# Self and cross attention of a fused block as one pipeline of four phases, with weights prepared a phase ahead

## The chip, the cores and the metric

The kernel runs on one core of a Trainium2 chip. The metric is the device time of one launch in microseconds (us). A core has five engines, each with its own queue of instructions that it works through in order: TensorE (PE, its weight loads shown as PEld), VectorE (DVE), ScalarE (ACT), GpSimd (POOL) and SyncE (SP), which here only starts transfers. An engine waits at an instruction until the semaphore that it names has reached a number, and everything behind that instruction waits with it.

## The reference

The input is 2048 tokens (32 sequences of 64) of 256 numbers. Five steps follow one another, the last four of them on a layer norm of the residual:

```
x = x + wkv(layernorm(x), ctx)                       # a recurrence along time
x = x + ternary_ffn(layernorm(x))                    # hidden 704, weights rounded to -1, 0, 1
x = x + attention(layernorm(x), ctx):                # 16 query heads, 8 key/value heads, head size 128
      q  = ln(fp8(h) @ wq)    k  = ln(fp8(h) @ wk)     v  = fp8(h) @ wv        # self
      qx = ln(fp8(h) @ wqx)   kx = ln(ctx @ wkx)       vx = ctx @ wvx          # cross
      cat = [softmax(q k^T / sqrt(128)) v, softmax(qx kx^T / sqrt(128)) vx]    # 32 heads
      out = fp8(cat / smooth) @ wproj * scale
x = x + routed_ffn(layernorm(x))                     # top 2 of 8, capacity 64
```

Keys and queries are normalised head by head. The mean over a head is taken out of the weights beforehand: every head's 128 weight columns of wq, wk, wqx and wkx are multiplied by their scale and then lose their mean ("centred"). Every weight is also split into two fp32r parts, upper and lower, whose products are added, which keeps the precision.

## The kernel before, in words

The stages run one after another, each a block with a barrier at its end: wkv, ternary FFN, the LN and quantisation stage that writes the fp8 activations `xq8`, self attention, cross attention, routed FFN.

**Weights before.** All six chunks of the self weights (q in two halves, k, v, the projection in two halves; 128 x 2048 each) are prepared during the ternary stage. ACT scales each head of q and k and sums it (`self_weights_act`, L653, 48 heads). POOL centres, copies the upper part and subtracts for the lower part (`self_weights_pool`, L664; the subtraction is in `lower_part`, L642, recorded as L645). Meanwhile DVE normalises `tf_z` (L812), rounds the ternary weights (L816 to L818), takes maxima (L825) and scales `tf_z` again (L831); the first unit of the ternary FFN (L851) comes behind all of that in DVE's queue. The cross weights are loaded during self attention; ACT and POOL scale and centre one head (`cross_head_act` L706, `cross_head_pool` L715) with six of every eight units. Splitting them into upper and lower parts is the start of the cross stage (`cross_weights_act` L723, `cross_weights_dve` L730), and TensorE waits for it at L1409.

**Attention.** Each of the two stages is a software pipeline over 64 units. A unit is one tile of 128 tokens (two sequences) and two key/value groups, so four query heads; four units make a tile. Step s of every engine works on units of different age. In TensorE's queue a step is: output products of unit s-4 (L1430, from `pT` and `v`), query transposes of s-2 (L1441), projection of s-5 (L1453, from `cat`), key and value products of s (L1417; L1477 in cross), key transposes of s-2 (L1487), query products of s (L1417 again), transposes of the probabilities of s-3 (L1499), scores of s-2 (L1507). ACT's step ends with the square of the query of s (L1394), `pT` (L1397), the copy of v (L1400) and, in self, the cross head (L711 and the read of its accumulator). DVE's step begins with the sum of squares of s-1 (L1251) and ends with `tb` of s-4 (L1292). POOL's step is: `pn` of s-3 (L1214), every fourth step the conversion of the next tile (L1195), `cat` of s-4 (L1228), and last the head (L718 for the sum, L720 for the weights). The projection gathers four units in PSUM; after every fourth DVE adds the tile to the residual (L1347). Steps are written once in a hardware loop of eight units, with the first round and the tail written out.

Of the kernel before, what the change touches and what calls it, by code (L numbers as in the profile page):

```python
# [100 lines left out]
def build_program(nc, x, ctxT, params, w1T, w3T, w2T, wqT, wkT, wvT, wqxT, wkvxT, wprojT, routerT,  # L101
                  fw1T, fw2T, fb2, out):
    ctx = ExitStack()
    with ctx:
# [26 lines left out]
        with ExitStack() as held:  # L131


            work = [sb(f"w_work{i}", [P, KC * G * D], F32, held) for i in range(3)]
            tok["tw"] = ternary_weights(tok, work, held)
            stage = tok["stage_sem"] = StageSems(nc)
            wkv_stage(tok, x, ctxT, params, (w1T, w3T, w2T))
            aw = attention_weights(tok, held)
            stage = tok["stage_sem"] = stage.follow()
            ternary_ffn_stage(tok, aw, self_chunks(tok, aw, wqT, wkT, wvT, wprojT))  # L140
            xq8 = sb("xq8", [P, 4 * KC, TOK], BF16, held)
            stage = tok["stage_sem"] = stage.follow()
            ln_quant_stage(tok, xq8, work)
            stage.follow()
            cross_w = cross_chunks(tok, aw, wqxT, wkvxT, wprojT)
            attention_stage(tok, "self", xq8, aw, work, cross_w, ctxT)
            attention_stage(tok, "cross", xq8, aw, work, cross_w, ctxT)
# [419 lines left out]

def attention_weights(k, stack):


    nc, sem = k["nc"], k["sem"]

    def pair(name, shape):
        return [stack.enter_context(nc.sbuf_tensor(f"{name}{p}", shape, F32R)) for p in range(2)]

    return dict(
        q=pair("wq", [P, KC, NH * D]), k=pair("wk", [P, KC, G * D]), v=pair("wv", [P, KC, G * D]),
        p=pair("wp", [P, NH, C]),
        sums=stack.enter_context(nc.sbuf_tensor("w_sums", [P, 3, NH], F32)),
        scales=stack.enter_context(nc.sbuf_tensor("w_scales", [P, 4 * KC], F32)),  # L580
        arrived=[sem(f"w_arrived{i}") for i in range(6)], scales_ready=sem("w_scales_ready"),
        sums_ready=sem("w_sums_ready"), scaled=sem("w_scaled"), centred=sem("w_centred"), upper=sem("w_upper"),
        lower_pool=sem("w_lower_pool"), lower_dve=sem("w_lower_dve"))


class Chunk:

    def __init__(self, pair, pick, src, centred=False, scales=()):  # L590
        self.src, self.centred, self.scales = src, centred, scales
        self.upper, self.lower = (pick(t) if len(pick(t).shape) == 2 else pick(t).rearrange("p a n -> p (a n)")
                                  for t in pair)

    def scale_of(self, head):
        return self.scales[head * len(self.scales) // NH]


def heads_of(w):
    return w.rearrange("p (h d) -> p h d", d=D)  # L600


def proj_chunks(aw, wprojT, row0):
    half = NH // 2
    return [Chunk(aw["p"], lambda t, a=a: t[:, a * half:(a + 1) * half, :],
                  wprojT[row0 + a * half * D:row0 + (a + 1) * half * D, :].rearrange("(c p) n -> p c n", p=P))
            for a in range(2)]


def self_chunks(k, aw, wqT, wkT, wvT, wprojT):  # L610
    def scale(kind, h):
        return aw["scales"][:, kind * KC + h:kind * KC + h + 1]

    def halves(w):
        return w.rearrange("(h p) n -> p h n", p=P)

    q = [Chunk(aw["q"], lambda t, h=h: t[:, h, :], wqT[h * P:(h + 1) * P, :], True, [scale(0, h)])
         for h in range(KC)]
    return q + [Chunk(aw["k"], lambda t: t[:], halves(wkT), True, [scale(1, h) for h in range(KC)]),
                Chunk(aw["v"], lambda t: t[:], halves(wvT), False, [scale(2, h) for h in range(KC)])  # L620
                ] + proj_chunks(aw, wprojT, 0)


def cross_chunks(k, aw, wqxT, wkvxT, wprojT):
    kv = wkvxT.rearrange("(h p) n -> p h n", p=P)
    q = [Chunk(aw["q"], lambda t, h=h: t[:, h, :], wqxT[h * P:(h + 1) * P, :], True,
               [aw["scales"][:, 3 * KC + h:3 * KC + h + 1]]) for h in range(KC)]
    return q + [Chunk(aw["k"], lambda t: t[:], kv[:, :, 0:G * D], True),
                Chunk(aw["v"], lambda t: t[:], kv[:, :, G * D:2 * G * D])] + proj_chunks(aw, wprojT, NH * D)


def load_weights(sp, aw, work, chunks, wait_free, first=0, last=6):
    for i in range(first, last):
        c = chunks[i]
        if i >= len(work):
            wait_free(i - len(work))
        w = work[i % len(work)][:]
        dst = w if len(c.src.shape) == 2 else w.rearrange("p (a n) -> p a n", a=c.src.shape[1])
        sp.dma_start(dst, c.src).then_inc(aw["arrived"][i], 16)


def lower_part(eng, aw, work, chunks, i, nth_upper, done):  # L642
    eng.wait_ge(aw["upper"], nth_upper + 1)
    c = chunks[i]
    eng.tensor_tensor(c.lower, work[i % len(work)][:], c.upper.bitcast(F32), ALU.subtract).then_inc(done, 1)  # L645

N_CHUNKS, N_CENTRED, N_SCALED = 6, 3, 4
CROSS_ON_DVE, CROSS_ON_POOL = (0, 1, 3), (2, 4, 5)  # L650


def self_weights_act(act, nc, aw, work, chunks):  # L653

    act.wait_ge(aw["scales_ready"], 4)
    for i, c in enumerate(chunks[0:N_CENTRED]):
        act.wait_ge(aw["arrived"][i], 16)
        for h in range(NH):
            head = heads_of(work[i][:])[:, h, :]
            last = nc.scalar.activation(head, head, ACT.Copy, scale=c.scale_of(h), accum_out=aw["sums"][:, i, h:h + 1])  # L660
# [3 lines left out]
def self_weights_pool(pool, nc, aw, work, chunks, col):  # L664
# [3 lines left out]
    for i, c in enumerate(chunks):  # L668
        w = work[i % len(work)][:]
        if c.centred:  # L670
            pool.wait_ge(aw["scaled"], i + 1)
            nc.gpsimd.tensor_scalar(aw["sums"][:, i, :], aw["sums"][:, i, :], -1.0 / D, None, ALU.mult
                                    ).then_inc(aw["sums_ready"], 1)
            pool.wait_ge(aw["sums_ready"], i + 1)
            nc.gpsimd.tensor_tensor(heads_of(w), heads_of(w),
                                    aw["sums"][:, i, :].unsqueeze(2).broadcast_to([P, NH, D]), ALU.add
                                    ).then_inc(aw["centred"], 1)
            pool.wait_ge(aw["centred"], i + 1)
        else:
            pool.wait_ge(aw["arrived"][i], 16)  # L680
            if c.scales:
                for h in range(KC):
                    half = w[:, h * G * D:(h + 1) * G * D]
                    last = nc.gpsimd.tensor_scalar(half, half, c.scales[h], None, ALU.mult)
                last.then_inc(aw["scaled"], 1)
                pool.wait_ge(aw["scaled"], i + 1)
        nc.gpsimd.tensor_copy(c.upper, w).then_inc(aw["upper"], 1)
        lower_part(nc.gpsimd, aw, work, chunks, i, i, aw["lower_pool"])


class CrossHead:


    PER_ROUND = 6
    WITH_UNITS = (1, 2, 3, 5, 6, 7)

    def __init__(self, aw, work, i, o):
        o = self.WITH_UNITS.index(o)
        self.chunk, self.first = o // 2, o % 2 == 0
        self.head = 2 * i + o % 2  # L700
        self.count = self.PER_ROUND * i + o + 1
        self.w = work[self.chunk][:, bass.ds(self.head * D, D)]
        self.sum = aw["sums"][:, self.chunk, bass.ds(self.head, 1)]


def cross_head_act(act, nc, aw, work, chunks, i, o):  # L706
    c = CrossHead(aw, work, i, o)
    if c.first and isinstance(i, int) and i == 0:
        act.wait_ge(aw["arrived"][c.chunk], 32)
    scales = chunks[c.chunk].scales  # L710
    nc.scalar.activation(c.w, c.w, ACT.Copy, scale=scales[0] if scales else 1.0, accum_out=c.sum  # L711
                         ).then_inc(aw["scaled"], 1)


def cross_head_pool(pool, nc, aw, work, minus_mean, i, o):  # L715
    c = CrossHead(aw, work, i, o)
    pool.wait_ge(aw["scaled"], N_SCALED + c.count)
    nc.gpsimd.tensor_tensor(c.sum, c.sum, minus_mean, ALU.mult).then_inc(aw["sums_ready"], 1)  # L718
    pool.wait_ge(aw["sums_ready"], N_CENTRED + c.count)
    nc.gpsimd.tensor_tensor(c.w, c.w, c.sum.broadcast_to([P, D]), ALU.add).then_inc(aw["centred"], 1)  # L720


def cross_weights_act(act, nc, aw, work, chunks):  # L723
    for i, c in enumerate(chunks):
        if not c.centred:
            act.wait_ge(aw["arrived"][i], 32)
# [1198 lines left out]
```

## Time and profile before

| | us |
|---|---|
| median of 3 runs | 1149.35 (1148.18 to 1149.48) |
| the profiled execution | 1150.45 |
| its span, first to last instruction | 1148.5 |
| busy in the span: PE, DVE, ACT, POOL | 890.5, 932.7, 715.9, 393.4 |
| mean granted TensorE clock | 0.883 of full speed |

The span is made of stages with different limits, so the shares of the whole span say little. A stage is read from its own stretch: who is busy in it without a gap, and what ended the waits of the engine that sets its end. A group in a timeline row is a run of equal instructions; its start, its length and, in brackets, the idle time ahead of it and what released the engine.

### The profile page before, as it was taken

The numbers are of one execution on the slowest core, as the hardware profiler recorded it, in microseconds if no ns is written. First come the engines' busy times: TensorE is split into PE (matmuls) and PEld (weight loads), VectorE is DVE, ScalarE is ACT, GpSimd is POOL, SyncE is SP. The second block draws the span as 40 slices with busy tenths as digits, with TensorE's granted clock in tenths as the row PEclk, the third lists the DMA queues.
The fourth block names the chain that finished last, engine by engine and source line by source line (L and its number), as shares of the span: only waits on it lengthen the run. The fifth ranks groups of instructions, "written<-read, shape, count | busy, mean of one in ns | idle before, by whom it ended". The sixth has DMA issues, their size and how long they took to land. (4 is left out here: it accounts for less than half of the span.)

```text
span 1148.5 us, 23844 instructions
## 1 busy us (share of the span) xinstructions
PE 890.5 (78%) x6878; PEld 787.9 (69%) x6878; DVE 932.7 (81%) x2442; ACT 715.9 (62%) x2471; POOL 393.4 (34%) x498
## 2 busy tenths in 40 slices
PE   3720056621899999999999369999999999997738
PEld 3710033321788888888898358999999999996627
DVE  7989989878889889989988448888888888886460
ACT  3445034363888888888888457777777777774303
POOL 0008910000344444444444433333343333323024
PEclk9865589855999999999999679999999999998559
DMA  6021200001100000000000220000000000000400
GB/s 223 1 100 50 70 0 1 0 0 67 45 2 1 0 0 0 0 0 0 0 0 1 60 69 6 11 6 5 5 9 5 5 5 5 0 0 1 152 19 19
DMA packets 18266, 26.96 MB, mean 23 GB/s; under 512 B 1264, under 2 KB 15408, under 8 KB 17456
## 3 DMA queue, kind: packets, MB, share of 16 engines
q1 hardware_dynamic: 17840, 25.41, 6.5%
q0 software_dynamic: 384, 1.05, 0.3%
q8 instruction: 19, 0.31, 0.1%
q14 instruction: 23, 0.19, 0.1%
HBM read 23.83 MB, written 2.62 MB: 23 GB/s over the span
## 5 line engine op out<-in xcount | busy, mean ns | idle before, releaser
L1214 POOL TENSOR_TENSOR c_pn<-c_p,c_rsum 128x256 f32<-128x256 f32 x64 | 39.6, 619 | 216.4 <-DVE c_rsum L1337 216.4
L1251 DVE TENSOR_REDUCE c_v<-c_sq 128x6 f32<-128x768 f32 x64 | 60.7, 949 | 54.4 <-ACT c_sq L1394 54.2
L1214 POOL TENSOR_TENSOR s_pn<-s_p,s_rsum 128x256 f32<-128x256 f32 x64 | 39.6, 618 | 141.0 <-DVE s_rsum L1337 141.0
L1228 POOL TENSOR_TENSOR s_cat<-s_tb,s_mb 128x512 fp32r<-128x512 bf16 x64 | 73.9, 1154 | 34.6 <-DVE s_tb L1292 34.6
L1251 DVE TENSOR_REDUCE s_v<-s_sq 128x6 f32<-128x768 f32 x64 | 60.7, 949 | 28.5 <-ACT s_sq L1394 28.1
L1228 POOL TENSOR_TENSOR c_cat<-c_tb,c_mb 128x512 fp32r<-128x512 bf16 x64 | 74.0, 1156 | 28.8 <-DVE c_tb L1292 28.8
L1453 PE MATMUL s_pj_ps<-wp,s_cat 128*128 128x256 f32 x512 | 78.9, 298 | 1.6 <-POOL s_cat L1228 1.6
L1453 PE MATMUL c_pj_ps<-wp,c_cat 128*128 128x256 f32 x512 | 78.1, 296 | 1.8 <-POOL c_cat L1228 1.8
L1377 ACT ACTIVATE s_p<-s_kT_sc_ps,s_nmax 128x64 f32<-128x64 f32 x256 | 76.6, 311 | 2.8 <-DVE s_nmax L1258 2.4
L1377 ACT ACTIVATE c_p<-c_kT_sc_ps,c_nmax 128x64 f32<-128x64 f32 x256 | 76.6, 311 | 2.7 <-DVE c_nmax L1258 1.8
L1417 PE MATMUL c_qo_ps<-wq,c_xqf 128*128 128x512 f32 x256 | 75.9, 419 | 0.0
L1417 PE MATMUL s_qo_ps<-wq,s_xqf 128*128 128x512 f32 x256 | 75.3, 416 | 0.0
L1477 PE MATMUL c_kv_ps<-wk,c_ctxp 128*128 128x256 f32 x384 | 57.3, 286 | 17.1 <-DVE wv L645 17.1
L1453 PEld LDWEIGHTS s_pj_ps<-wp,s_cat 128*128 128x128 f32 x512 | 67.0, 195 | 3.2 <-POOL s_cat L1228 1.9
L1453 PEld LDWEIGHTS c_pj_ps<-wp,c_cat 128*128 128x128 f32 x512 | 66.3, 193 | 4.1 <-issue 2.1
L1417 PE MATMUL s_kv_ps<-wk,s_xqf 128*128 128x256 f32 x256 | 41.6, 285 | 32.5 <-POOL s_xqf L1195 32.5
L1507 PE MATMUL s_kT_sc_ps<-s_kT,s_qT 128*128 128x64 f32 x512 | 64.4, 269 | 1.0 <-ACT s_kT L1390 1.0
L1507 PE MATMUL c_kT_sc_ps<-c_kT,c_qT 128*128 128x64 f32 x512 | 64.3, 269 | 0.0
L1507 PEld LDWEIGHTS s_kT_sc_ps<-s_kT,s_qT 128*128 128x128 f32 x512 | 62.2, 192 | 1.7 <-ACT s_qT L1382 1.0
L1477 PEld LDWEIGHTS c_kv_ps<-wk,c_ctxp 128*128 128x128 f32 x384 | 51.0, 193 | 17.5 <-DVE wv L645 17.4
L1507 PEld LDWEIGHTS c_kT_sc_ps<-c_kT,c_qT 128*128 128x128 f32 x512 | 62.3, 192 | 0.2
L948 PE MATMUL tf_xT_ps<-identb,tf_xq 128*128 128x128 bf16 x32 | 4.8, 234 | 71.0 <-DVE tf_cur L853 71.0
(359 smaller groups left out, 2912.8 us busy)
## 6 DMA issues: line engine op xcount, KB each, us to landing
x_res<-in_x SPq DMA_DIRECT2D x4, 512.0 KB, 6.0
vT<-in_ctxT SPq DMA_DIRECT2D x2, 1024.0 KB, 10.5
tf_work<-in_wqT SPq DMA_DIRECT2D x2, 1024.0 KB, 6.2
tf_work<-in_wprojT SPq DMA_DIRECT2D x2, 1024.0 KB, 5.5
w_work<-in_wqxT SPq DMA_DIRECT2D x2, 1024.0 KB, 6.6
w_work<-in_wkvxT SPq DMA_DIRECT2D x2, 1024.0 KB, 8.1
c_ctx<-in_ctxT SPq DMA_DIRECT2D x16, 128.0 KB, 2.2
w_work<-in_wprojT SPq DMA_DIRECT2D x2, 1024.0 KB, 7.9
```

Source lines behind the costliest of these rows:

```text
L948: last = nc.tensor.transpose(xT_ps[:, h * P:(h + 1) * P], xq[par][:, h * P:(h + 1) * P], identb[:])
L1214: nc.gpsimd.tensor_tensor(pn[:].rearrange("p (a t) -> p a t", a=4), pe_s[:].rearrange("p (a t) -> p a t", a=4), rsum[:].unsqueeze(2).broad ...
L1228: nc.gpsimd.tensor_tensor(cat[out8.o % 2][:], tb[:], mb[:], ALU.subtract).then_inc(cat_ready, 1)
L1251: norm(nc.vector.tensor_reduce(v6[:], sq[:].rearrange("p (h d) -> p h d", d=D), AX.X, ALU.add))
L1377: nc.scalar.activation(pe_s[:, a * S:(a + 1) * S], sc_ps[:, a * S:(a + 1) * S], ACT.Exp, bias=nmax[:, a:a + 1], accum_out=psum_s[:, a:a + ...
L1417: last = nc.tensor.matmul(out_ap, x_col(h), w_pair[part][:, h, c0:c1], start=(n == 0), stop=(n == 2 * KC - 1))
L1453: last = nc.tensor.matmul(pj_ps[:, 0:C], cat[pj.o % 2][:, a * P:(a + 1) * P], wp[part][:, gpj * HU + a, :], start=(gpj == 0 and a == 0 and ...
L1477: last = nc.tensor.matmul(kv[:, c:c + KW], ctx_p[tp][xp][:, h, :], w[wpart][:, h, cols], start=(n == 0), stop=(n == 3 * KC - 1))
L1507: last = nc.tensor.matmul(sc_ps[:, a * S:(a + 1) * S], qT[:, a * P:(a + 1) * P], kT[:, g * P + b * S:g * P + (b + 1) * S], start=True, sto ...
```

## The change

The two attention stages become one, of 128 units in four phases of 32: self attention with the first half of the heads over all 16 tiles, self with the second half, cross first half, cross second half. A unit is what it was; two of them now make a tile of a phase (`turn`), the projection of two tiles gathers in two halves of one PSUM bank, and DVE adds two tiles at once, again once in four units. Tiles are converted by POOL once in two units, not four. All steps are written out, with no hardware loop.

There are two sets of weight buffers, each for half of the heads. The ternary stage prepares phase 0's half alone: 24 heads on ACT; on POOL v and the projection first, then q and k. Phase p prepares phase p+1's half: 24 heads (scaled and summed on ACT, centred on POOL) with the units 1 to 24 of the phase, and 24 pieces of 128 x 256 (upper on ACT at units 5 to 28, lower on DVE at 6 to 29). TensorE waits at a phase's first unit for all pieces. In ACT's step head and piece come last; in POOL's step the head stands between `pn` and `cat`, and the conversion behind `cat`. On TensorE the query transposes go ahead of the output products. In DVE's step `round8` and `newton` alternate, the reciprocal L1337 is ahead of the last `newton` part, and the residual add is ahead of the normalised key. SP loads the next half's raw weights when the pieces of the current one are lowered; phase 1's q is loaded in the LN stage.

```diff
+def first_weights_pool(pool, nc, aw, raw, col):
...
+    split("v", 1)
+    pool.wait_ge(aw["arrived"]["p"], 16)
+    split("p", 2)
...
+    for nth, (part, n) in enumerate((("q", KC * QC // D), ("k", KC * KVC // D))):
...
+FIRST_HEAD_AT, FIRST_UPPER_AT, FIRST_LOWER_AT = 1, 5, 6
...
+        def head_item(u):
+
+            i = u.o - FIRST_HEAD_AT
+            return Head(aw, raw_w, u.phase + 1, i) if u.phase + 1 < N_PHASES and 0 <= i < N_HEADS else None
...
+                for s in range(UNITS + 4):
+                    u, soft, out8 = At(s), At(s - 3), At(s - 4)
                     if soft.live:
...
-                    if u.live and o % UT == 0:
...
-                            convert(nxt, par, i + 1 if par else i + 2)
+                    head = head_item(u) if u.live else None
+                    if head:
+                        pool.wait_ge(aw["head_scaled"], head.count)
+                        nc.gpsimd.tensor_tensor(head.sum, head.sum, minus_mean[:], ALU.mult).then_inc(aw["head_sum"], 1)
+                        pool.wait_ge(aw["head_sum"], head.count)
+                        nc.gpsimd.tensor_tensor(head.w, head.w, head.sum.broadcast_to([P, D]), ALU.add
+                                                ).then_inc(aw["head_centred"], 1)
                     if out8.live:
-                        pool.wait_ge(cadd_ready, out8.count(1, 1))
+                        pool.wait_ge(cadd_ready, out8.count())
                         wait_unit(pool, pj_done, out8.before(2))
-                        nc.gpsimd.tensor_tensor(cat[out8.o % 2][:], tb[:], mb[:], ALU.subtract).then_inc(cat_ready, 1)
-                    if own_kv and u.live and o in CrossHead.WITH_UNITS:
-                        cross_head_pool(pool, nc, aw, work, minus_mean[:], i, o)
+                        nc.gpsimd.tensor_tensor(cat[out8.n % 2][:], tb[:], mb[:], ALU.subtract).then_inc(cat_ready, 1)
+                    if u.live and u.half == 0 and u.turn + 1 < N_PHASES * NT:
+                        wait_unit(pool, kv_done, u.before(1))
+                        wait_unit(pool, q_done, u.before(1))
+                        convert(u.turn + 1)
...
                     if u.live:
                         wait_unit(act, pv_done, u.before(4))
-                        nc.scalar.activation(v_s[u.o % 4][:], kv_bank(u)[:, KW:2 * KW], ACT.Copy).then_inc(v_ready, 1)
...
+                        nc.scalar.activation(v_s[u.n % 4][:], kv_bank(u)[:, KW:2 * KW], ACT.Copy).then_inc(v_ready, 1)
+                        head = head_item(u)
+                        if head:
+                            if head.first:
+                                act.wait_ge(aw["arrived"][head.part], 16 * (u.phase + 2))
+                            nc.scalar.activation(head.w, head.w, ACT.Copy, scale=head.scale, accum_out=head.sum
+                                                 ).then_inc(aw["head_scaled"], 1)
+                        w, _ = piece(u, FIRST_UPPER_AT)
...
+                    if now.live:
+                        w, count = piece(now, FIRST_LOWER_AT)
+                        if w:
+                            dve.wait_ge(aw["piece_upper"], count)
...
+                        if u.o == 0 and u.phase:
+                            pe.wait_ge(aw["piece_lower"], N_PIECES * u.phase)
```

## Rows read from the trace of the kernel before

**Rows 1.** Busy time by stretch: length, PE, PEld, DVE, ACT, POOL, granted clock, DMA.
```profile
160.00:170.00 10.00, 6.85 (x50) 4.07 (x50) 9.58 (x27) 4.87 (x13) 0.00 (x0) 1.00 0.00 0
...
400.00:500.00 100.00, 99.46 (x805) 89.03 (x804) 89.74 (x259) 82.83 (x319) 44.54 (x70) 1.00 0.00 0
```

**Rows 2.** Timeline of PE: start, length, engine, line, what, how many, [idle before].
```profile
309.75 0.66 PE L1441 MATMUL s_qT_ps<-ident,s_qn 128*128 128x128 f32 x4
...
626.43 0.66 PE L1441 MATMUL s_qT_ps<-ident,s_qn 128*128 128x128 f32 x4
...
631.50 1.12 PE L1441 MATMUL s_qT_ps<-ident,s_qn 128*128 128x128 f32 x4
...
677.55 1.11 PE L1441 MATMUL c_qT_ps<-ident,c_qn 128*128 128x128 f32 x4 [6.27 <-DVE c_qn L1297]
```

**Rows 3.** Timeline of PE, one self unit from projection to projection.
```profile
616.17 1.19 PE L1453 MATMUL s_pj_ps<-wp,s_cat 128*128 128x256 f32 x8
...
618.27 1.17 PE L1417 MATMUL s_qo_ps<-wq,s_xqf 128*128 128x512 f32 x4
...
621.54 1.19 PE L1453 MATMUL s_pj_ps<-wp,s_cat 128*128 128x256 f32 x8
```

**Rows 4.** Timeline of DVE ahead of the ternary FFN's first unit.
```profile
80.42 5.25 DVE L812 TENSOR_SCALAR tf_z<-x_res,mean,rstd 128x256 f32<-128x256 f32 x16
85.71 0.95 DVE L816 TENSOR_SCALAR w_work<-w_work,iws 128x1408 f32<-128x1408 f32 x1
...
112.93 4.40 DVE L825 TENSOR_REDUCE tf_amax<-tf_z 128x16 f32<-128x4096 f32 x1
...
123.71 25.10 DVE L831 TENSOR_SCALAR tf_z<-tf_z,tf_qs 128x256 f32<-128x256 f32 x16
```

**Rows 5.** Timeline of POOL, the same stretch.
```profile
113.20 3.61 POOL L675 TENSOR_TENSOR tf_work<-tf_work,w_sums 128x2048 f32<-128x2048 f32 x1
...
123.32 5.87 POOL L684 TENSOR_SCALAR tf_work<-tf_work,w_scales 128x1024 f32<-128x1024 f32 x2
...
142.14 1.95 POOL L687 CAST wp<-tf_work 128x2048 fp32r<-128x2048 f32 x1
144.17 4.49 POOL L645 TENSOR_TENSOR wp<-tf_work,wp 128x2048 fp32r<-128x2048 f32 x1
```

**Rows 6.** Timeline of ACT: the first head of the self weights.
```profile
82.57 0.40 ACT L660 ACTIVATE tf_work<-tf_work,w_scales 128x128 f32<-128x128 f32 x1 [2.95 <-DMA tf_work<-in_wqT]
```

**Rows 7.** Timeline of POOL in the unit of rows 3.
```profile
619.64 1.16 POOL L1228 TENSOR_TENSOR s_cat<-s_tb,s_mb 128x512 fp32r<-128x512 bf16 x1 [0.66 <-DVE s_tb L1292]
620.98 0.19 POOL L718 TENSOR_TENSOR w_sums<-w_sums,s_minus_mean 128x1 f32<-128x1 f32 x1 [0.18 <-ACT w_work L711]
621.25 0.40 POOL L720 TENSOR_TENSOR w_work<-w_work,w_sums 128x128 f32<-128x128 f32 x1
```

**Rows 8.** Timeline of ACT, its head in that unit; line L711's min/median/max ns.
```profile
620.49 0.32 ACT L711 ACTIVATE w_work<-w_work  x1
620.69 0.21 ACT L711 ACTIVATION_READ_ACCUMULATOR w_work<-w_work  x1
...
L711 ACT ACTIVATE w_work<-w_work,w_scales x32: 402/412/420, 288.9 to 615.1; - x28, 128x128 f32<-128x128 f32 x4
```

**Rows 9.** POOL's `cat` and the projection waiting for it, self's end.
```profile
643.82 1.15 POOL L1228 TENSOR_TENSOR s_cat<-s_tb,s_mb 128x512 fp32r<-128x512 bf16 x1 [2.83 <-DVE s_tb L1292]
...
645.03 2.08 PE L1453 MATMUL s_pj_ps<-wp,s_cat 128*128 128x256 f32 x8 [1.61 <-POOL s_cat L1228]
```

**Rows 10.** Timeline of PE in cross: query products and the next projection.
```profile
844.84 1.17 PE L1417 MATMUL c_qo_ps<-wq,c_xqf 128*128 128x512 f32 x4
...
848.11 1.19 PE L1453 MATMUL c_pj_ps<-wp,c_cat 128*128 128x256 f32 x8
```

**Rows 11.** Timeline of DVE: `tb` beside POOL's conversion; a lower part.
```profile
433.67 1.03 DVE L1292 TENSOR_TENSOR s_tb<-s_yb,s_mb 128x512 bf16<-128x512 bf16 x1
...
661.81 2.29 DVE L645 TENSOR_TENSOR wv<-w_work,wv 128x2048 fp32r<-128x2048 f32 x1 [5.61 <-ACT wv L727]
```

More of the change, by code:

```diff
@@ L599, in heads_of @@
[L599 to L621, printed above, removed]
@@ L624, in cross_chunks @@
[L624 to L639, printed above, removed]
@@ L642, in lower_part @@
[L642 to L653, printed above, removed]
-    act.wait_ge(aw["scales_ready"], 4)
[L656 to L660, printed above, removed]
+        lower=sem("w_lower"), head_scaled=sem("w_head_scaled"), head_sum=sem("w_head_sum"),
@@ L667, in self_weights_pool @@
                                 ALU.mult).then_inc(aw["scales_ready"], 1)
[L668 to L678, printed above, removed]
-        else:
[L680 to L688, printed above, removed]
@@ L691 @@
[L691 to L712, printed above, removed]
@@ L715, in cross_head_pool @@
[L715 to L726, printed above, removed]
-        nc.scalar.activation(c.upper, work[i % len(work)][:], ACT.Copy).then_inc(aw["upper"], 1)
@@ new lines, with __init__ @@
+class Head:
+    def __init__(self, aw, raw, phase, i):
+        self.part, per = ("q", QC // D) if i < KC * QC // D else ("k", KVC // D)
+        h, a = divmod(i if self.part == "q" else i - KC * QC // D, per)
+        self.w = raw[self.part][:, h, a * D:(a + 1) * D]
+        self.sum = aw["sums"][:, i:i + 1]
+        self.first = h == 0 and a == 0
+        kind = {"q": 0, "k": 1}[self.part] if phase < 2 else {"q": 3, "k": None}[self.part]
+        self.scale = 1.0 if kind is None else scale_col(aw, kind, h)
+        self.count = N_HEADS * (phase - 1) + i + 1
@@ new lines, with __init__ @@
+N_PIECES = KC * (QC + 2 * KVC) // PIECE + PR
+class Piece:
+    def __init__(self, aw, raw, sets, phase, m):
+        self.first = False
+        for self.part, n in (("v", KC * KVC // PIECE), ("p", PR), ("q", KC * QC // PIECE), ("k", KC * KVC // PIECE)):
+            if m < n:
+                break
+            m -= n
+        self.first = m == 0
+        if self.part == "p":
+            at = (slice(None), m, slice(None))
+        else:
+            h, c = divmod(m, n // KC)
+            at = (slice(None), h, slice(c * PIECE, (c + 1) * PIECE))
+        self.raw = raw[self.part][at]
+        self.upper, self.lower = (t[at] for t in sets[phase % 2][self.part])
+        self.scale = scale_col(aw, 2, h) if self.part == "v" and phase < 2 else None
```

439 lines of the change are left out of this document (252 added, 187 removed).

## The prediction, made before the changed kernel ran

> **What bounds the kernel now.** I read the windows by stage first. In self attention TensorE is busy 99.46 of 100 us at full granted clock while DVE has 89.74 [rows 1]: in the steady part TensorE's own work is the bound, and moving work about between the other engines gains nothing there. So the change can win only outside that part, and lose only by making TensorE wait. Next, the timeline of TensorE by its query transposes, one group per unit. A self unit takes 5.37 us (projection to projection in rows 3), but from 309.75 to 626.43 there are 58 units, a mean of 5.46 [rows 2]. Between self's last query transposes (631.50) and cross's first (677.55) lie 46.05 us [rows 2]: the drain, the barrier, the splitting of the cross weights and the refill. Last, the ternary stage's start: DVE is never idle from 80.42 until its second pass over `tf_z` ends at 148.81 (123.71 + 25.10), and the FFN's first unit stands behind that pass. The pass takes 25.10 us; the first one, with as many operations of the same size, took 5.25 before POOL had begun [rows 4]. POOL's last subtraction ends at 148.66 [rows 5]. So POOL's weight preparation slows DVE down and sets that end.
>
> **Part 1, half of the weights in the ternary stage.** POOL's new series from rows 5: v scaled 2.94 (half of 5.87), v split 0.97 + 2.25 (halves of 1.95 and 4.49), projection split 1.95 + 4.49, q centred and split 3.61 + 1.95 + 4.49, k half of that 5.03, two small operations some 0.6: 28.3 us. v is half the size of the transfer whose data released ACT at 82.57 [rows 6], so I let POOL begin at 81.3; some 4 us go to the wait for the projection's transfer and to DVE operations in its way: POOL ends near 113. In the old stretch about one DVE operation got through per POOL instruction (29 beside 20). With 16 POOL instructions, the first of them beside the short operations of the first pass, DVE should be through with rounding the weights when POOL ends, and have left the reduction 4.40, a second pass of 5.25 and some 1 us of small ones [rows 4]: end near 124.5, gain 24 us. Bounds: DVE undisturbed, 80.42 + 5.25 + twelve rounding operations of at most 0.95 + 4.40 + 1 + 5.25 = 107.7, gain 41; four rounding operations left over, gain 20. I take 24, since the trace shows the disturbance. ACT's 24 heads instead of 48 end earlier and are hidden; SP issues fewer bytes and now waits for nothing.
> The trace shows a pass of short DVE operations at a fifth of its speed beside POOL [rows 4, 5]. The Trainium skill (SBUF — State Buffer, "SBUF: two separate sides") says that the two engines' shared port pair is an exclusive lock, held for a whole instruction. By it DVE would get one gap per POOL instruction, 16 of some 22 operations in POOL's time, so up to 6 of 0.95 left over and a gain of 18 instead of 24.
>
> **Part 2, the seam.** The 46.05 us become one ordinary unit of 5.84: -40.2. TensorE's new wait for all pieces costs nothing: the last piece is lowered at unit 29 of 32. The loads (1 MB, issued three units or more ahead) are hidden by those units.
>
> **Part 3, ordinary stalls.** 58 x (5.46 - 5.37) = 5.2 us go today to `tb` being held for 1.03 us by POOL's conversion [rows 11] together with the residual add, which makes `pn` late. The conversion moves behind `cat`, the reciprocal ahead. With about 1 us of loop turns in cross I take -6; between -7 and 0. The doubled conversions fall into POOL's free time (44.54 of 100 busy [rows 1]). ACT's upper piece comes after the head in its step, ahead of the next logarithm, and that has slack in either case. DVE's lower piece is 2.29/8 = 0.29 us [rows 11], covered by the 10 us in 100 that DVE has free and by what the interleaving returns; without the cover it is a rival below. Longer setup and a residual add of two tiles at the end: +0.6.
>
> **Part 4, the head ahead of `cat`.** This decides. POOL's step s is now `pn`, head of unit s, `cat` of s-4. ACT scales that head as one of the last things of its step s, behind the query square, `pT` and v, so behind TensorE's query products of the same unit. And TensorE's step s+1 has the projection from that `cat` *ahead* of its own key, value and query products. That closes a loop with one turn per unit: query products, ACT's head, POOL's head, `cat`, next projection, next query products. Today the head stands behind `cat`, and no engine waits for it.
> From the start of the query products, 618.27 [rows 3]: ACT's head starts at 2.22 and its sum is read by 2.63 (620.69 + 0.21 [rows 8]); POOL's sum starts at 2.71, the head's weights at 2.98, their end is at 3.38 [rows 7]. Then `cat`, 1.16 [rows 7]: 4.54, with no allowance for the handover (the projection that did wait for `cat` began 0.06 after its end [rows 9]; POOL's back-to-back instructions overlap by as much). Today the projection starts at 3.27 (621.54 [rows 3]); `cat` was ready at 2.53 (620.80 [rows 7]). So TensorE waits 1.27 us. Heads with a scale take ACT 0.412 instead of 0.32 [rows 8]: 1.36. In cross the interval is 3.27 as well (844.84 to 848.11 [rows 10]), so the same price. Behind the projection TensorE is the bound again and cannot catch up: each unit with a head becomes 6.64 or 6.73 us long in self, 7.1 or 7.2 in cross.
> How many: 24 heads in each of phases 0, 1 and 2. In phase 0 the first projection is in step 5, so heads 1 to 3 cost nothing: 21 scaled. Phase 1 prepares the cross weights, q scaled (16), k not (8); phase 2 the same. 53 x 1.36 + 16 x 1.27 = 72.1 + 20.3 = 92.4. Bounds: 69 x 1.2 = 83 (handovers shorter) and 69 x 1.5 = 104 (the exposed weight load, a POOL operation held by DVE).
> What is queued behind the wait: `cat`, the conversion, the next `pn`. The last two are in time even 1.4 us late, as TensorE needs `pn` only after its query products.
>
> **Sum.** -24 - 40.2 - 6 + 0.6 + 92.4 = +22.8. The profiled execution took 1150.45 around a span of 1148.5, so a span of 1171.3 and an execution of 1173; against the median of 1149.35, 1172. With the ends together: -41 - 40.2 - 7 + 83 = -5, and -18 - 40.2 + 1 + 104 = +47.
>
> **Rivals.**
> A, the other side: the loop does not bite and it is faster. It decides at 3.27 us from query products to `cat`'s end; ACT's part alone uses 2.63 and `cat` 1.16, 3.79 together [rows 3, 7, 8], so it bites even if POOL's head were free. For it speaks only that TensorE never waited for `cat` in the steady part today, by 0.74 us, and that I read the order from the text. 1149.35 - 24 - 40.2 - 6 + 1 = 1080.
> B, DVE becomes a second bound where there is no head: pieces at 0.29, a residual add of twice the width, and POOL's conversions twice as often, each able to hold a DVE operation for half a microsecond or more [rows 11]. At 0.3 us in each of the 128 - 69 = 59 units without a wait, +18: 1190. Against it: most pieces fall into units with a head, where DVE gets 1.3 us more.
> By the same page of the skill a DVE operation with two SBUF inputs, as the lower part is, is also held by POOL; that would be B.
> C, the clock: TensorE idle for 1.3 us in 6.7 could lose the granted clock. With the 2.1 us from projection to query products doubled, 69 x 2.1 = +145: 1317. Against it: in the ternary stage it was granted 1.00 while busy 6.85 of 10 us [rows 1], and here it is busy 80%.
> D, only part of the wait shows, since ACT gets to the head earlier than today: at half the price, -46: 1126.
>
> **How the numbers follow.** Forecast (the sum within its ends) 0.73, A 0.10, B 0.08, C 0.02, D 0.07. The forecast's own range is 1144 to 1196. That alone holds about 0.7 and B most of its 0.08, so the range is 1142 to 1198. No change, within 0.2% (2.3 us, about what a measurement here can tell), needs the ends together: 0.03. Faster: A, D and the rest of the low end, 0.20. Slower 0.77.
>
> **What would show it.** Ternary: the FFN's first `tf_xq` near 124 instead of 149. Seam: no gap at a phase's start. Loop: units of 6.6 to 6.8 us in three quarters of phases 0 and 1 and 7.1 to 7.3 in phase 2, a wait of the projection for `cat` of 1.2 to 1.4 us, some 69 times, and POOL waiting for ACT's head ahead of it; 5.4 us in the last eight units of phases 0 and 1, 5.8 in phase 3. Wrong if the projection finds `cat` ready, or if the waits in steps with a head end on another engine.

## The result, and the profile after

| | before | after |
|---|---|---|
| median | 1149.41 us (1148.18 to 1149.74, 4 runs) | 1186.05 us (1183.49 to 1187.53, 4 runs) |
| span of the profiled execution | 1148.5 | 1184.0 |
| mean granted TensorE clock | 0.883 | 0.898 |

The changed kernel is slower: ratio 1.0318, 95% interval 1.0299 to 1.0338, inside the range and on the side forecast, 14 us above the forecast of 1172. The page of the kernel after, parts 1 and 5 (busy time, mean of one in ns, idle time just ahead and its releaser):

```profile
PE 894.8 (76%) x6878; PEld 785.4 (66%) x6878; DVE 957.7 (81%) x2509; ACT 723.2 (61%) x2536; POOL 401.2 (34%) x602
...
L1477 PE MATMUL a_pj_ps<-wp,a_cat 128*128 128x256 f32 x1024 | 157.6, 297 | 91.8 <-POOL a_cat L1231 91.8
...
L1224 POOL TENSOR_TENSOR w_sums<-w_sums,a_minus_mean 128x1 f32<-128x1 f32 x72 | 13.7, 190 | 237.9 <-ACT w_work L1418 237.9
```

One line carries the result: TensorE stood 91.8 us ahead of the projection, for `cat`; and POOL, ahead of the head's sum, stood 237.9 us for ACT's head. The stretch that had TensorE busy 99.46 of 100 us [rows 1], from the windows of the kernel after:

```profile
400.00:500.00 100.00, 88.16 (x713) 79.19 (x714) 86.51 (x245) 75.06 (x289) 40.27 (x58) 1.00 0.07 23
```

No engine is now busy all the time: this is a loop of handovers, not an engine at its limit. The loop itself, from the timelines of PE, ACT, DVE and POOL in one unit of phase 0 after (start, length, ..., [idle before <- releaser]):

```profile
333.30 1.22 PE L1477 MATMUL a_pj_ps<-wp,a_cat 128*128 128x256 f32 x8 [1.32 <-POOL a_cat L1231]
...
335.44 1.18 PE L1443 MATMUL a_qo_ps<-wq,a_xqf 128*128 128x512 f32 x4
...
340.08 1.21 PE L1477 MATMUL a_pj_ps<-wp,a_cat 128*128 128x256 f32 x8 [1.31 <-POOL a_cat L1231]
```
```profile
336.65 0.60 ACT L1407 ACTIVATE a_sq<-a_qo_ps 128x512 f32<-128x512 f32 x1 [0.31 <-PE a_qo_ps L1443]
...
337.67 0.41 ACT L1418 ACTIVATE w_work<-w_work,w_scales 128x128 f32<-128x128 f32 x1
337.96 0.21 ACT L1418 ACTIVATION_READ_ACCUMULATOR w_work<-w_work,w_scales 128x1 f32 x1
```
```profile
336.16 0.42 DVE L1293 TENSOR_TENSOR a_tb<-a_yb,a_mb 128x512 bf16<-128x512 bf16 x1
```
```profile
338.25 0.19 POOL L1224 TENSOR_TENSOR w_sums<-w_sums,a_minus_mean 128x1 f32<-128x1 f32 x1 [3.42 <-ACT w_work L1418]
338.52 0.40 POOL L1226 TENSOR_TENSOR w_work<-w_work,w_sums 128x128 f32<-128x128 f32 x1
338.88 1.15 POOL L1231 TENSOR_TENSOR a_cat<-a_tb,a_mb 128x512 fp32r<-128x512 bf16 x1
```

The query products start at 335.44. ACT squares them when they are done and gets to its head at 337.67. DVE has `tb` ready at 336.58, and with it POOL could have begun `cat`; instead it waits for the head, 3.42 us in all, and then does the head and `cat` (end 340.03), and the projection starts 0.05 later. From query products to projection it is 4.64 us, where rows 3 have 3.27. The projection stands ahead of the next query products in TensorE's queue, and so the turn closes. The waits from 300 to 1080 us count them (total, times, longest):

```profile
POOL w_sums L1224 <- ACT w_work L1418: 216.9, 66, 5.4
...
PE a_pj_ps L1477 <- POOL a_cat L1231: 85.8, 68, 1.3
```

The ternary stage, timeline of DVE after, to be held against rows 4:

```profile
80.76 10.95 DVE L791 TENSOR_SCALAR tf_z<-x_res,mean,rstd 128x256 f32<-128x256 f32 x16
...
118.06 4.40 DVE L804 TENSOR_REDUCE tf_amax<-tf_z 128x16 f32<-128x4096 f32 x1
...
123.28 4.29 DVE L810 TENSOR_SCALAR tf_z<-tf_z,tf_qs 128x256 f32<-128x256 f32 x16
127.60 0.29 DVE L830 TENSOR_SCALAR tf_xq<-tf_z 128x256 bf16<-128x256 f32 x1
```

The second pass is down from 25.10 to 4.29 us, the first one up from 5.25 to 10.95, since POOL now begins early. The first `tf_xq` is at 127.60 (before: 148.85).

Where the +35.5 us of span come from, read from the first query transposes of each phase. Timeline of PE after:

```profile
269.08 0.66 PE L1457 MATMUL a_qT_ps<-ident,a_qn 128*128 128x128 f32 x4 [0.80 <-DVE a_qn L1298]
...
469.28 0.61 PE L1457 MATMUL a_qT_ps<-ident,a_qn 128*128 128x128 f32 x4
...
675.44 0.61 PE L1457 MATMUL a_qT_ps<-ident,a_qn 128*128 128x128 f32 x4
...
898.86 0.61 PE L1457 MATMUL a_qT_ps<-ident,a_qn 128*128 128x128 f32 x4
...
1079.64 0.60 PE L1457 MATMUL a_qT_ps<-ident,a_qn 128*128 128x128 f32 x4
```

The same five points of before are 289.35, 463.31, 677.55, 865.41 and 1045.91. Attention starts 20.3 us earlier, takes 810.56 instead of 756.56 (+54.0), and what follows its last query transposes is 1.8 us longer: -20.3 + 54.0 + 1.8 = +35.5. By phases after: 200.2, 206.2, 223.4, 180.8; before: 174.0, 214.2 with the seam in it, 187.9, 180.5. The three phases that carry heads pay; phase 3, which prepares nothing, does not.

### The profile page after: what moved, and what is told of

The parts are those of the page before. It is cut to its first block and busy times, and to the rows that moved or that the text cites. A ratio compares the mean times of both kernels' runs of the same rounds, so it can differ in the third digit from the quotient of the medians.

```text
span 1184.0 us, 22559 instructions
## 1 busy us (share of the span) xinstructions
PE 894.8 (76%) x6878; PEld 785.4 (66%) x6878; DVE 957.7 (81%) x2509; ACT 723.2 (61%) x2536; POOL 401.2 (34%) x602
## 5 line engine op out<-in xcount | busy, mean ns | idle before, releaser
L1477 PE MATMUL a_pj_ps<-wp,a_cat 128*128 128x256 f32 x1024 | 157.6, 297 | 91.8 <-POOL a_cat L1231 91.8
L1254 DVE TENSOR_REDUCE a_v<-a_sq 128x6 f32<-128x768 f32 x128 | 121.8, 951 | 116.1 <-ACT a_sq L1407 115.9
L1477 PEld LDWEIGHTS a_pj_ps<-wp,a_cat 128*128 128x128 f32 x1024 | 131.0, 192 | 112.5 <-POOL a_cat L1231 105.9
L1231 POOL TENSOR_TENSOR a_cat<-a_tb,a_mb 128x512 fp32r<-128x512 bf16 x128 | 147.6, 1153 | 63.5 <-DVE a_tb L1293 61.5
L1389 ACT ACTIVATE a_p<-a_kT_sc_ps,a_nmax 128x64 f32<-128x64 f32 x512 | 151.5, 307 | 2.9 <-DVE a_nmax L1261 2.9
L1443 PE MATMUL a_qo_ps<-wq,a_xqf 128*128 128x512 f32 x512 | 151.2, 417 | 0.0
L1535 PE MATMUL a_kT_sc_ps<-a_kT,a_qT 128*128 128x64 f32 x1024 | 128.8, 269 | 0.6 <-ACT a_kT L1403 0.6
L1535 PEld LDWEIGHTS a_kT_sc_ps<-a_kT,a_qT 128*128 128x128 f32 x1024 | 124.3, 192 | 1.2 <-ACT a_qT L1395 1.0
L1389 ACT ACTIVATION_READ_ACCUMULATOR a_p<-a_kT_sc_ps,a_nmax 128x1 f32 x512 | 103.3, 202 | 0.0
L1395 ACT ACTIVATE a_qT<-a_qT_ps,a_lnp 128x512 f32<-128x512 f32 x128 | 101.0, 789 | 0.0
L1224 POOL TENSOR_TENSOR w_sums<-w_sums,a_minus_mean 128x1 f32<-128x1 f32 x72 | 13.7, 190 | 237.9 <-ACT w_work L1418 237.9
```

Of the source, the lines that this page charges most:

```text
L1231: nc.gpsimd.tensor_tensor(cat[out8.n % 2][:], tb[:], mb[:], ALU.subtract).then_inc(cat_ready, 1)
L1254: norm(nc.vector.tensor_reduce(v6[:], sq[:].rearrange("p (h d) -> p h d", d=D), AX.X, ALU.add))
L1389: nc.scalar.activation(pe_s[:, a * S:(a + 1) * S], sc_ps[:, a * S:(a + 1) * S], ACT.Exp, bias=nmax[:, a:a + 1], accum_out=psum_s[:, a:a + ...
L1395: nc.scalar.activation(qT[:], qT_ps[:], ACT.Identity, scale=lnp[:, i, 0:1], bias=lnp[:, i, 1:2]).then_inc(qT_ready, 1)
L1443: last = nc.tensor.matmul(out_ap, x_col(h), w_pair[part][:, h, c0:c1], start=(n == 0), stop=(n == 2 * KC - 1))
L1477: last = nc.tensor.matmul(pj_ps[:, pj.turn % 2, :], cat[pj.n % 2][:, a * P:(a + 1) * P], wp[part][:, pj.half * HU + a, :], start=(pj.half ...
```

## The experiments

Times of a table row are medians; the ratio is to the kernel before, whose median beside the first four was 1148.69 (7 runs), beside the next four 1149.22 (9) and beside the last two 1150.37 (9).

| | us | ratio to before, 95% |
|---|---|---|
| e1 head behind `cat` | 1092.2 | 0.9506 [0.9474, 0.9537] |
| e2 before, head ahead of `cat` | 1214.4 | 1.0572 [1.0535, 1.0609] |
| e3 head one unit late | 1090.1 | 0.9486 [0.9455, 0.9517] |
| e4 ACT's head early | 1094.1 | 0.9516 [0.9485, 0.9547] |
| e6 old DVE order | 1094.3 | 0.9521 [0.9497, 0.9545] |
| e7 conversion ahead of `cat` | 1090.6 | 0.9493 [0.9471, 0.9516] |
| e8 ACT centres the first weights | 1083.4 | 0.9424 [0.9406, 0.9441] |
| e9 after once more | 1188.0 | one run |
| e10 residual add behind `tb` | 1084.4 | 0.9432 [0.9419, 0.9445] |
| e11 and the piece behind it | 1083.7 | 0.9418 [0.9405, 0.9431] |

**e1, the loop undone by order.** POOL's head goes behind `cat` and the conversion, all else as after.

```diff
-                    head = head_item(u) if u.live else None
-                    if head:
-                        pool.wait_ge(aw["head_scaled"], head.count)
-                        ...
                     if out8.live:
                         ...
                         nc.gpsimd.tensor_tensor(cat[out8.n % 2][:], tb[:], mb[:], ALU.subtract).then_inc(cat_ready, 1)
                     if u.live and u.half == 0 and u.turn + 1 < N_PHASES * NT:
                         ...
                         convert(u.turn + 1)
+                    head = head_item(u) if u.live else None
+                    if head:
+                        ...
```

> The changed kernel with one edit: POOL's head stands last in its step, behind cat and the conversion. Loop theory: the projection's waits for cat (91.8 us in the changed kernel) go, the two 3 us stretches at half clock too; units with a head shrink from 6.78 and 7.25 us to 5.4 and 5.87, 69 times 1.37 = 94 us and 3 us of clock: 1186 - 97 = 1089 us. Rival DVE: the pieces and the wider residual add are the load that matters, and DVE becomes the bound as soon as the wait is gone: units with a piece stay at 5.7 us or more in self, some 1105 to 1120 us.

1092.2 us. Units with a head are 5.40 or 5.6 us in self and 5.87 in cross; the windows of e1 have TensorE full again:

```profile
400.00:500.00 100.00, 99.70 (x809) 89.77 (x807) 92.67 (x274) 84.84 (x325) 45.79 (x68) 1.00 0.05 17
```

The order of two items in POOL's queue is worth 94 us, and without it the change is 5% faster than before.

**e2, the loop put into the kernel before.** The only edit: the head goes ahead of `cat`.

```diff
+                    if own_kv and u.live and o in CrossHead.WITH_UNITS:
+                        cross_head_pool(pool, nc, aw, work, minus_mean[:], i, o)
                     if out8.live:
                         ...
                         nc.gpsimd.tensor_tensor(cat[out8.o % 2][:], tb[:], mb[:], ALU.subtract).then_inc(cat_ready, 1)
-                    if own_kv and u.live and o in CrossHead.WITH_UNITS:
-                        cross_head_pool(pool, nc, aw, work, minus_mean[:], i, o)
```

> The kernel before with one edit: in self attention POOL's head (six of every eight units, 48 in all) stands ahead of cat, not behind it. Loop theory: 45 of the 48 heads stand beside a live projection, 45 times 1.3 = 59 us, less up to 5 us of today's stalls that vanish into the wait: 1149 + 54 to 59 = 1203 to 1208 us. Rival, that the order on POOL matters only through the 0.6 us of the head's own work ahead of cat, of which 0.74 us of slack covers all: 1149 to 1155 us.

1214.4 us: +65.7 for 48 heads, 1.37 each, above the 54 to 59 that were expected. Two of the units with a head took 8.3 us where the others take 6.6 to 7.0; in both the granted clock was 0.50 for some 3 us behind the wait for `cat`. The windows of e2 (columns as in rows 1):

```profile
312.00:315.00 3.00, 3.00 (x16) 3.00 (x15) 2.02 (x9) 0.40 (x1) 0.61 (x1) 0.50 0.00 0
339.50:342.50 3.00, 3.00 (x16) 3.00 (x15) 1.88 (x7) 0.00 (x0) 0.61 (x1) 0.50 0.02 5
```

That is some 3 us of the excess; the rest was not taken apart. The waits of e2 from 289 to 640 us name the same pair:

```profile
POOL w_sums L718 <- ACT w_work L711: 115.2, 41, 7.3
...
PE s_pj_ps L1453 <- POOL s_cat L1230: 48.3, 38, 1.3
```

So the place of the head alone makes the loss, in either kernel, and nothing else of the change is needed for it.

**e3, same place and work, another unit's head.** If POOL's place or its work ahead of `cat` were the cost, this would not help; if the dependence within the unit is, it goes.

```diff
-                    head = head_item(u) if u.live else None
+                    late = At(s - 1)
+                    head = head_item(late) if late.live else None
```

> The changed kernel with one edit: POOL's head is still ahead of cat, but it is that of the unit one step back, which ACT scaled a whole step ago. The work on POOL and its place are the same; only the wait is satisfied beforehand. Loop theory: as with the head behind cat, 1089 us, within 5. Rival, that the place and POOL's work in front of cat cost: stays at 1186, or at least above 1130.

1090.1 us: the head's 0.6 us still stand ahead of `cat`, and cost nothing. What cost the 96 us between the kernel after and e3 (some 3 of them the clock's, see e9) was that the head came from this unit's query products.

**e4, the same loop shortened at its other end.** ACT scales the head ahead of the squares, so ahead of its wait for the query products; POOL as after.

```diff
+                        head = head_item(u)
+                        if head:
+                            ...
+                            nc.scalar.activation(head.w, head.w, ACT.Copy, scale=head.scale, accum_out=head.sum
+                                                 ).then_inc(aw["head_scaled"], 1)
                         ...  # squares, kT, pT, v
-                        head = head_item(u)
-                        ...
```

> The changed kernel with one edit: POOL as it was (head ahead of cat, same unit), but ACT scales the head ahead of the squares in its step, where it does not stand behind TensorE's query products. Loop theory: the chain from the query products to the head is cut at its other link, so the waits go as well: 1089 us, up to 10 more if ACT's 0.5 us makes the squares late in units without slack. Rival place and work on POOL: above 1130.

1094.1 us. Three different cuts, on POOL's order, on the unit's index and on ACT's order, remove the same 92 to 96 us. POOL in e4 does the head at once behind `pn`, then has 0.7 us to spare ahead of `cat`:

```profile
336.65 0.19 POOL L1224 TENSOR_TENSOR w_sums<-w_sums,a_minus_mean 128x1 f32<-128x1 f32 x1
336.92 0.40 POOL L1226 TENSOR_TENSOR w_work<-w_work,w_sums 128x128 f32<-128x128 f32 x1
338.01 1.16 POOL L1231 TENSOR_TENSOR a_cat<-a_tb,a_mb 128x512 fp32r<-128x512 bf16 x1 [0.70 <-DVE a_tb L1293]
```

**e6 and e7, Part 3's two reasons one by one, on e1.** e6 puts DVE's small operations back into their old order, e7 POOL's conversion ahead of `cat`.

```diff
-                    if u.live:
-                        newton(0)
                     if pv.live:
                         round8(1)
                     if u.live:
-                        newton(1)
+                        newton(0)
                     if pv.live:
                         round8(2)
+                    if u.live:
+                        newton(1)
+                        newton(2)
                     ...
```

> e1 (head behind cat and conversion, 1092.2) with DVE's round8 and newton parts in the order of the kernel before, the reciprocal behind the last newton part as there. Theory of Part 3 (the reciprocal behind makes pn late, and TensorE's probability transposes wait for it): stalls of about 0.1 us a unit come back, 1096 to 1105. Rival (TensorE is the bound by enough, or DVE's order doesn't matter): 1090 to 1094.

> e1 (1092.2) with POOL's conversion ahead of cat, as before. Theory of Part 3 (the conversion holds tb, and cat and the next step come late): every second unit grows by 0.1 to 0.4 us over e1's, 1095 to 1105, with tb at about 1.0 us in these units. Rival: in e1 every second self unit is 0.22 us longer because the conversion behind cat holds DVE's small operation ahead of the maximum (0.72 instead of 0.17 us); ahead of cat it no longer does, the excess goes, and the time is 1085 to 1090.

The times of neither are told apart from e1's: 1094.3 (1091.9 to 1096.3) and 1090.6 (1089.2 to 1092.5) against 1092.2. In the traces, one of each, attention takes 718.7 us in e6, 718.1 in e1 and 716.8 in e7, between the first and the last query transposes: the old DVE order costs 0.6, the old place of the conversion gains 1.3. My second reason, that the conversion behind `cat` spares a stall, fell; if anything it is the other way about. In e7's self phases every second one of e1's units of 5.6 us is back at 5.40, as the rival had it, while every fourth unit of the third phase grew from 5.87 to 5.98.

**e8, less POOL in the ternary stage.** On e3. ACT, which is through with its 24 heads at 94.40, centres the first q and k heads and copies their upper parts; POOL keeps v, the projection and the lower parts.

```diff
+    act.wait_ge(aw["sums_ready"], KC + 1)
+    ...
+                last = nc.scalar.activation(head, head, ACT.Identity, bias=aw["sums"][:, at:at + 1])
+    ...
+        nc.scalar.activation(aw["sets"][0][part][0][:], raw[part], ACT.Copy).then_inc(aw["centred"], 1)
...
-        for h in range(KC):
-            nc.gpsimd.tensor_tensor(heads[:, h], heads[:, h],
-                                    ...
-        split(part, 3 + nth)
+        nc.gpsimd.tensor_tensor(lower, raw[part], upper.bitcast(F32), ALU.subtract).then_inc(aw["lower"], 1)
```

> The kernel after with two edits: POOL's head is that of the unit before, as in e3 (1090.1), and in the ternary stage ACT, idle from 94.41, centres the 24 heads (0.39 us each, 9.4 in all) and copies the upper parts of q and k; POOL keeps v, the projection and the two lower subtractions (5.0 and 2.4 us). Theory of Part 1 (POOL's two-input instructions hold DVE's): 8.1 us of centring and 3.9 of copies leave POOL, it is free from 97 to about 105, DVE gets its rounding done by some 107, the reduction of 4.40 ends near 111, the second pass near 117, so the first tf_xq comes near 117 instead of 127.6: 1090 - 10 = 1080 (1077 to 1085). Rival (DVE slow by itself or on ACT's account, or the end is set by the weights arriving): tf_xq stays at 124 to 128 and the time at 1087 to 1090.

1083.4 us, 6.7 under e3, and the fastest of all with e10 and e11; the first `tf_xq` comes at 120.55, not 117. Timeline of DVE in e8, and under it POOL's:

```profile
97.75 0.89 DVE L800 TENSOR_SCALAR w1q<-w_work 128x1408 bf16<-128x1408 f32 x1
98.56 0.95 DVE L798 TENSOR_SCALAR w_work<-w_work,iws 128x1408 f32<-128x1408 f32 x1
...
103.80 4.62 DVE L798 TENSOR_SCALAR w_work<-w_work,iws 64x256 f32<-64x256 f32 x1
108.45 2.31 DVE L799 TENSOR_SCALAR w_work<-w_work 64x256 f32<-64x256 f32 x1
```
```profile
96.01 0.90 POOL L672 TENSOR_SCALAR w_sums<-w_sums 128x24 f32<-128x24 f32 x1
103.76 4.51 POOL L676 TENSOR_TENSOR wq<-tf_work,wq 128x2048 fp32r<-128x2048 f32 x1 [6.85 <-ACT wq L648]
108.22 2.40 POOL L676 TENSOR_TENSOR wk<-tf_work,wk 128x1024 fp32r<-128x1024 f32 x1
```

While POOL is idle (96.91 to 103.76) DVE's rounding operations take 0.83 to 0.95 us each. The next one is tiny, 64 x 256, and takes 4.62 beside a POOL instruction of 4.51; the one behind it takes 2.31 beside one of 2.40; the third of that size, at 110.80 with POOL idle again, takes 0.29. So two small DVE operations were held as long as the POOL instruction beside them ran. The Trainium skill (SBUF — State Buffer, "SBUF: two separate sides") says of the shared port pair that whichever of the two starts first, a DVE operation in a 2-port mode or a GpSimd operation, has it for the whole instruction and blocks the other; these two rows agree with it. A case in which nothing was held stands in the last section.

**e9, the kernel after once more**, for its two units of 8.77 and 8.69 us in phase 2.

> The kernel after once more, for the two units of 8.7 us in phase 2 in which the granted clock fell to 0.50. Were they due to something at a fixed place (a transfer, one unit's work), they come at the same two units again, about 1186. Were they due to the clock taking a wait of 1.3 us for idleness by chance, they come at other units or in another number, 1181 to 1190.

1188.0 us. This time three units are 1.5 us longer than their neighbours, at other places: one each in phases 0, 1 and 2 (8.31, 8.31 and 8.79). No fixed place, so not a transfer or one unit's work. In the kernel after, windows around the first (length, PE, PEld, DVE, ACT, POOL, granted clock, DMA):

```profile
718.00:720.00 2.00, 2.00 (x23) 1.80 (x20) 1.28 (x3) 1.93 (x7) 0.27 (x2) 1.00 0.00 0
720.00:722.00 2.00, 0.68 (x7) 0.52 (x4) 1.94 (x7) 1.97 (x11) 1.43 (x2) 0.90 0.00 0
722.00:724.00 2.00, 2.00 (x11) 2.00 (x11) 1.55 (x5) 0.19 (x1) 0.61 (x1) 0.50 0.00 0
724.00:726.00 2.00, 2.00 (x14) 1.96 (x14) 1.26 (x4) 0.33 (x2) 0.00 (x0) 0.75 0.00 0
```

After the 1.32 us wait that ends at 721.48 the granted clock is 0.50, the lower of its two levels (1.2 GHz of 2.4), for some 3 us. What that costs shows in the timeline of PE, the key products one unit earlier and these:

```profile
715.28 0.87 PE L1505 MATMUL a_kv_ps<-wk,a_ctxp 128*128 128x256 f32 x6
...
723.27 1.48 PE L1505 MATMUL a_kv_ps<-wk,a_ctxp 128*128 128x256 f32 x6
```

**e10 and e11, where the remaining excess sits.** In e3 and e8 every fourth self unit is 5.60, not 5.39. e10 (on e8) moves DVE's residual add of two tiles from ahead of `tb` to behind it; e11 moves the lower piece behind `tb` as well.

```diff
-                    if pj.live and pj.n % 4 == 3:
-                        ...                               # the residual add
                     if u.live:
                         normalised_key()
+                    if pv.live:
+                        round8(3)                         # e11 only; in e10 it stays behind the piece
                     if now.live:
                         ...                               # the lower piece
-                    if pv.live:
-                        round8(3)                         # e11 only
+                    if pj.live and pj.n % 4 == 3:
+                        ...
```

> e8 (1083.4) with DVE's residual add of two tiles moved from ahead of the normalised key to behind tb. Theory, formed on e3's and e8's units (5.40, 5.40, 5.40, 5.60 in self): the add, 0.66 us once in four units, makes tb late, cat and the projection behind it by 0.2, and this is where the stalls that Part 3 took off came back; with the add behind tb the excess goes from some 16 self units: 0.21 x 16 = 3.4, 1080. Rival (the excess comes from POOL's conversion beside DVE's small operation, 0.37 instead of 0.17 us, or the add then delays the next sum of squares as much): 1083 to 1085.

> As e10, with tb ahead of the normalised key's piece too: the lower subtraction, 0.33 us in 24 units of a phase, is then behind tb as well, and cat starts 0.33 us earlier. Theory: with the add gone from ahead of tb, cat has slack already, so nothing more: the same as e10 within 1 us. Rival (the piece is part of the excess, B of the prediction): another 1 to 4 us less.

Both as fast as e8; the gain of 3.4 us that I expected did not come. In e3 the projection found `cat` 0.2 us late in these units:

```profile
PEld a_pj_ps L1478 <- POOL a_cat L1232: 4.1, 12, 0.3
```

That wait is gone in e11 (in the same stretch, 320 to 600 us, no wait of TensorE for `cat` is named), yet the excess stays: 5.75 in the units with an add in e10, about 5.54 in every second unit in e11. It ends only in the last eight units of a phase, which carry no head: 5.37 to 5.41 in e11, while e3 and e10 still have 5.60 there as long as pieces are lowered. So the theory of e10 fell: `tb` behind the add was where the stall showed, not all of its cause, and while heads, pieces and adds share a step, moving one of them moved the stall. Which chain then carries it (DVE's sum of squares, ACT's logarithm, the maximum) I have not settled. The traces point at DVE. Two of its steps in e3, from one sum of squares to the next, the first with the residual add:

```profile
385.65:391.29 5.64, 5.64 (x48) 5.13 (x48) 5.50 (x17) 5.17 (x21) 2.16 (x4) 1.00 0.00 0
391.29:396.65 5.36, 5.22 (x44) 4.65 (x43) 5.17 (x17) 4.59 (x19) 3.15 (x6) 1.00 0.01 5
```

In the long step DVE is idle for 0.14 us, and in the long ones of e10 and e11 for 0.1 to 0.2; once e3's pieces are done, a step without an add leaves it 0.7 to 0.8 us, and the units are 5.4 us. No run took work off DVE here, so this is not shown.

## Why the prediction was right, and where it was off

The terms, as forecast and as measured. e3 stands for "the change without the loop" (its phases: 172.3, 175.1, 187.9, 180.8); with e1 in its place the stalls would be +1.7 and the loop 89.5:

| term | forecast | measured | from |
|---|---|---|---|
| ternary stage | -24 | -20.3 | first query transposes, 289.35 to 269.08 |
| seam | -40.2 | -40.2 | 46.05 against 5.85 at the phase change |
| ordinary stalls | -6 | -0.3 | e3 against before, seam apart |
| loop | +92.4 | +91.5 | phases after less e3's, 94.5, less the clock's 3.0 |
| clock | 0 | +3.0 | two units, 1.5 each |
| ends | +0.6 | +1.8 | behind the last query transposes |
| sum | +22.8 | +35.5 | |

**Part 4, the loop**, was right in mechanism, place, count and size: units with a scaled head 6.78 (forecast 6.73), unscaled 6.68 (6.64), cross 7.25 and 7.17 (7.2 and 7.1), 5.4 to 5.6 in the last eight units of phase 0 and in six of those of phase 1 (the other two already hold cross's first products and take 5.85), 5.86 in phase 3, and the wait 68 times from 300 to 1080 us, at up to 1.32 us. What made it predictable is that every leg has a row in the trace of before, although the loop itself is not there. e1, e3 and e4 show it by cutting it, e2 by making it. Rival A (it does not bite) and D (half of it) fell.

**Part 2, the seam**, came out as forecast to the tenth of a microsecond: nothing at the start of a phase waits for the pieces.

**Part 1, the ternary stage**, is a term mis-sized. POOL began at 82.51 instead of 81.3, and its own instructions were longer beside DVE's rounding than the rows that I had added up: scaling v 3.61 us (2.94), centring q 4.99 in two halves (3.61 in one, beside DVE's reduction, in rows 4 and 5), the lower part of q 5.02 (4.49), k's centring and copy 3.09 and 1.51 (1.8 and 0.97). The trace of before had such rows too: its first centring, copy and lower part of q, beside the rounding, took 4.19, 2.43 and 4.96. The series took 35.2 us, not the 28.3 plus 4 that I allowed, and ended at 117.7, not 113. Of the rounding only one operation, of 0.29 us, was then left over, so the step that was off is POOL's end and not the count of DVE's operations. The gain came out at 21.25 at the first `tf_xq`, and another 1.0 was lost on the way to attention. The sum by the Trainium skill (SBUF — State Buffer, "SBUF: two separate sides") had been 18, so the trace lies between the two. e8 shows the cause: take 12 us of POOL's work out and DVE is 7 us earlier. It also shows the limit: the two subtractions that POOL keeps there each held a DVE operation.

**Part 3, ordinary stalls**, is the step that failed: -6 forecast, -0.3 measured. The old stalls did go (per eight self units before there is one of 5.65 and one of 5.88, the latter in the round's last unit; from 320 to 600 us TensorE's weight loads wait for `pn` 37 times in before, 12.5 us, and in e3 not at all), and others took their place: each unit of phase 0 is 5.40 instead of 5.37, one in four is 5.60, and the cross units are 5.86 to 5.88 instead of 5.83. What I had put at nothing is what the change puts ahead of `tb`: the lower pieces, named at 0.29 us and called covered by the 10 us in 100 that DVE has free, and the residual add of two tiles. A piece measured 0.42 to 0.58 us in e3, the add 0.74 where one tile takes 0.47. Of Part 3's two reasons e7 refuted the conversion's, and e6 found 0.6 us in DVE's order. In size it is rival B in small, 0.2 us in every fourth unit or so instead of 0.3 in all; that DVE is the bound there is likely, not shown. DVE's busy share rises from 89.74 of 100 [rows 1] to 93.17 in e3. A stall removed by order came back elsewhere, in e10 and e11 once more, against my own second guess.

**The clock**, rival C, I had put at all or nothing. It did neither: of some 69 waits of 1.3 us two (in the repeat three) were followed by 3 us at the lower level. That is 3 to 4.5 us. In e2 it was two as well.

Of the 14 us that the median lies above the forecast, stalls make 5.7, the ternary stage 3.7, the clock 3.0 and the ends 1.2; the loop takes 0.9 off. That is 12.7. Most of the other 1.3 comes from the medians, which differ by 36.6 us where the spans of the two profiled executions differ by 35.5. All errors but the loop's had the same sign. The two terms that came out within 1 us, seam and loop, are the ones whose mechanism the runs bear out.

## What to carry to other kernels

Before an item is moved in an engine's queue, ask what it waits for and what stands behind it; if the first comes late in a step and the second is needed early in the next, the move closes a loop that costs every step, however small the item (0.6 us of POOL work cost 92 us here, and the same work for the unit before cost nothing). Each leg's length can be read from the old trace even when the loop isn't in it, and add them before anything else. And where a second engine is nearly full (DVE had 89.7 of 100 us before the change and 93.2 in e3), do not count a removed stall as gone until that engine's new work in the same step is added up, at the durations that it has there.

## What the runs showed of the hardware

- A wait of TensorE of 1.2 to 1.3 us in a unit of 6.8 or 7.2 us was followed, two or three times in 69 and at places that changed between runs, by some 3 us at half the granted clock (0.50); in e2 twice in 38, there behind waits of 1.17 and 1.12 us. In the kernel after such a unit is 1.5 us longer.
- A DVE operation of 64 x 256 took 4.62 us beside one POOL subtraction of 4.51 (e8). Not every POOL instruction holds DVE so. In the kernel after, POOL scales v in two operations while DVE is in its first pass over `tf_z`; the timeline of POOL, and the part of DVE's pass beside it (min/median/max ns):

```profile
82.51 3.61 POOL L655 TENSOR_SCALAR tf_work<-tf_work,w_scales 128x512 f32<-128x512 f32 x2 [3.08 <-DMA tf_work<-in_wvT]
```
```profile
L791 DVE TENSOR_SCALAR tf_z<-x_res,mean,rstd x8: 400/544/768, 82.4 to 85.6; 128x256 f32<-128x256 f32 x8
```

  Undisturbed such an operation takes 0.41 us; beside the two scalings of 1.99 and 1.64 none took more than 0.77. The last three of the pass took as long as what POOL did beside them: 1.18 us beside a copy of 1.04, 2.51 beside a subtraction of 2.35, and 1.97 beside a copy of 1.95. There a copy, with one input, holds DVE as a subtraction does, and the scaling did not.
- It goes both ways: POOL's centring of 128 x 2048, as two halves, took 4.99 us beside DVE's rounding in the kernel after; in before it took 4.19 as one operation beside the rounding and 3.61 beside DVE's reduction [rows 4, 5].
